# A two-layer graph convolution network: in the first convolution's dense groups, edge attributes become the weights of the matmul and the one-hot table streams past them

## What is computed

```python
def conv(h, W, b):
    m = jnp.concatenate([h[dst], h[src], edge_attr], axis=1) @ W + b
    return jax.ops.segment_sum(m, dst, num_segments=n_nodes)
h = jax.nn.relu(conv(x, W1, b1))
```

## Time and profile before

| | |
|---|---|
| median of 3 runs | 8141.34 us |
| lowest and highest | 8137.03 and 8143.66 us |
| the profiled execution | 8128.06 us |
| its span | 8126.3 us |
| TensorE busy in the span | 6793.0 us (84%) |
| VectorE busy | 4444.9 us (55%) |
| ScalarE busy | 2307.4 us (28%) |
| mean granted clock of TensorE | 0.891 |

### The profile page before, as it was taken

How to read it: one execution, slowest core, us unless ns; L and a number is a source line. 1 busy time by engine, 2 the same in 40 slices (tenths; PEclk the granted TensorE clock), 3 DMA queues, 4 the chain that set the end, 5 groups by cost and what they waited for, 6 DMA issues and landing times. The chain is left out here.

```text
span 8126.3 us, 167963 instructions
## 1 busy us (share of the span) xinstructions
PE 6793.0 (84%) x53896; PEld 5553.6 (68%) x53897; DVE 4444.9 (55%) x5962; ACT 2307.4 (28%) x3815; POOL 5634.3 (69%) x5891
## 2 busy tenths in 40 slices
PE   5999999889997898895788788887868788888886
PEld 4777777788886888885666666665656566666664
DVE  7888886322222222225666666666566666566566
ACT  4878876100000000002222222222232222222223
POOL 4666664477775777774777777777557777777774
PEclk9999998688887888897999998888989889898897
DMA  5666666477776777773222222222232222222222
GB/s 183 238 236 244 236 239 205 167 269 278 284 277 227 287 282 269 272 262 113 72 67 68 72 67 72 68 70 69 59 84 70 70 67 71 69 71 67 72 72 70
DMA packets 415308, 1226.32 MB, mean 151 GB/s; under 512 B 120178, under 2 KB 219852, under 8 KB 366574
## 3 DMA queue, kind: packets, MB, share of 16 engines
q1 hardware_dynamic: 214343, 743.70, 25.6%
q0 software_dynamic: 187712, 233.42, 13.3%
q10 hardware_dynamic: 13160, 248.08, 7.6%
HBM read 943.22 MB, written 281.51 MB: 151 GB/s over the span
## 5 line engine op out<-in xcount | busy, mean ns | idle before, releaser
L1947 POOL DMA_INDIRECT data<-q_rows,idx x3328 | 3160.2, 950 | 1123.5 <-issue 1001.3
L922 POOL DMA_INDIRECT data<-h_parts,idx x2508 | 2427.6, 968 | 1202.3 <-issue 1019.6
L1054 PE MATMUL p_z<-hs,adj 128*128 128x192 bf16 x22442 | 2115.6, 252 | 61.5 <-issue 61.5
L1054 PEld LDWEIGHTS p_z<-hs,adj 128*128 128x128 bf16 x22442 | 1934.6, 100 | 313.4 <-issue 105.3
L2079 ACT COPY back<-p_back 128x1024 f32<-128x1024 f32 x418 | 423.3, 1013 | 2375.2 <-PE p_back L1967 2375.2
L2149 DVE TENSOR_TENSOR_SCAN run<-reset,run,p_turn 128x1024 f32<-128x1024 bf16 x416 | 974.5, 2342 | 147.2 <-PE p_turn L2014 142.8
L1169 ACT CAST adj<-p_count 128x1012 bf16<-128x1012 f32 x836 | 920.0, 1101 | 213.3 <-PE p_count L1040 190.0
L575 DVE TENSOR_TENSOR hot<-p_ramp,ends 128x2048 f32<-128x2048 f32 x416 | 950.0, 2284 | 0.5 <-issue 0.4
L1973 PE MATMUL part<-hot,t 128*128 128x128 f32 x6688 | 910.3, 295 | 44.9 <-issue 44.9
L1973 PEld LDWEIGHTS part<-hot,t 128*128 128x128 f32 x6688 | 879.1, 212 | 45.5 <-issue 45.5
L1978 PE MATMUL part<-hot,back 128*128 128x128 f32 x6688 | 815.1, 275 | 0.0
(11 more groups left out here) (324 smaller groups left out, 6381.9 us busy)
## 6 DMA issues: line engine op xcount, KB each, us to landing
adj<-counted SPq DMA_DIRECT2D x304, 1568.0 KB
counted<-adj ACTq DMA_DIRECT2D x76, 3136.0 KB
reset<-flags SPq DMA_DIRECT2D x208, 512.0 KB
data<-q_rows,idx POOLq DMA_INDIRECT x3328
data<-h_parts,idx POOLq DMA_INDIRECT x2508
feat<-in_ea_blocks SPq DMA_DIRECT2D x208, 128.0 KB
ea<-in_ea_cols SPq DMA_DIRECT2D x154, 88.0 KB
rden<-node_rows SPq DMA_DIRECT2D x50, 256.0 KB
```

Of the source, the lines that this page charges most:

```text
L922: pool.indirect_dma_start(out=data[:, p % HELD, j, 0:PARTS], out_offset=None, in_=table[:, :], in_offset=bass.IndirectOffsetOnAxis(ap=idx[ ...
L1054: mm = pe.matmul(p_z[:, 0:PARTS], adj[:, (q + LAG) % 2, hi, :], hs[:, hi, :], start=(hi == 0), stop=(hi == BLOCKS - 1))
L1947: pool.indirect_dma_start(out=data[:, r, j, :], out_offset=None, in_=q_rows[:, :], in_offset=bass.IndirectOffsetOnAxis(ap=idx[:, r, j:j + ...
```

## The change

In an E group of the first convolution, the operands of the eleven products change places. The attributes (`dense_ea`, 128 edges by 49) are the weights now, and the one-hot table (128 edges by 128 places) streams. The result comes out with features in partitions and places in columns, as `acc` has it, into columns 3P to 4P of the bank of `p_part`. Nothing is left to turn: the copy of ScalarE, the matmul L946 and its waits are gone, and `finish` waits for the products (`s_part`) and reads them where they are. `s_by_feature` is now counted by P groups alone. The P groups and the two later convolutions do what they did. What `further_products` does for edges outside the window is as it was.

```diff
             def products(pos, slot, halfway=None):
                 par = nth[pos] % 2
+                if slot is None:
+                    for j in range(GC):
+                        mm = pe.matmul(p_turned[0:EA, 3 * P:4 * P], dense_ea[:, j, 0:EA], hot[:, par, j, :],
+                                       start=(j == 0), stop=(j == GC - 1))
+                    return mm
                 for j in range(GC):
                     if halfway and j == HALFWAY:
                         halfway()
-                    mm = pe.matmul(p_part[:, columns(pos)], hot[:, par, j, :],
-                                   rows_of_edges(pos, slot, j), start=(j == 0), stop=(j == GC - 1))
+                    mm = pe.matmul(p_part[:, 0:WIDE], hot[:, par, j, :],
+                                   data[:, slot % HELD, j, :], start=(j == 0), stop=(j == GC - 1))
                 return mm
...
-            def by_feature(n):
+            def by_feature():
 
-                if hots[n] not in POS_P:
-                    return pe.matmul(p_turned[0:EA, 2 * P:3 * P], by_place[:, D:], chip.ident[:, :], start=True, stop=True)
                 return pe.matmul(p_turned[0:M, 2 * P:3 * P], by_place[:, 0:M], chip.ident[:, :], start=True, stop=True)
...
             def turn(k, pos):
                 n = nth[pos]
-                if pos in POS_E:
-                    pe.wait_ge(s_by_place, k * NQ + (POS_E.index(pos) + 2))
-                else:
-                    pe.wait_ge(s_by_sum, k * len(POS_P) + ((POS_P.index(pos) if pos >= 0 else -1) + 2))
+                pe.wait_ge(s_by_sum, k * len(POS_P) + (nth_p[pos] + 2))
...
                         if first:
                             between[2] = lambda pos=pos: by_window(k, pos, None)
-                            between[5] = lambda pos=pos: turn(k, pos)
...
                 for i in range(GC):
                     m = q * GC + i
-                    if i == 4:
-                        copy_places(k, POS_E[q])
...
-            def copy_places(k, pos):
-                n = nth[pos]
-                act.wait_ge(s_part, k * H + (H + n + 1))
-                act.wait_ge(s_by_feature, k * H + (n + 1 + BEFORE))
-                gate(act)
-                nc.scalar.copy(by_place[:, D:], p_part[:, PARTS:PARTS + EA]).then_inc(s_by_place, 1)
...
                 to = acc[rows, window(base, 0)]
-                v.wait_ge(s_by_feature, k * H + (n + 2 + BEFORE))
+                if pos in POS_E:
+                    v.wait_ge(s_part, k * H + (H + n + 1))
+                else:
+                    v.wait_ge(s_by_feature, k * len(POS_P) + (nth_p[pos] + 2 + BEFORE))
...
-                v.tensor_tensor(to, to, p_turned[0:at, 2 * P:3 * P], ALU.add).then_inc(s_added, 1)
+                of = slice(3 * P, 4 * P) if pos in POS_E else slice(2 * P, 3 * P)
+                v.tensor_tensor(to, to, p_turned[0:at, of], ALU.add).then_inc(s_added, 1)
```

More of the change, by code:

```diff
@@ L686, in conv_pass @@
     nth[-1] = -1
+    nth_p = {pos: n for n, pos in enumerate(POS_P)}
+    nth_p[-1] = -1
     M = KC if first else D
@@ L928, in _ @@
         def _(pe):
-            columns = lambda pos: slice(0, WIDE) if pos in POS_P else slice(PARTS, PARTS + EA)
-            def rows_of_edges(pos, slot, j):
-                return data[:, slot % HELD, j, :] if slot is not None else dense_ea[:, j, 0:EA]
             def products(pos, slot, halfway=None):
                 par = nth[pos] % 2
+                if slot is None:
[3 more added lines that the diff above has]
+                    return mm
                 for j in range(GC):
@@ L998, in turn @@
                 n = nth[pos]
-                if pos in POS_E:
-                    pe.wait_ge(s_by_place, k * NQ + (POS_E.index(pos) + 2))
-                else:
-                    pe.wait_ge(s_by_sum, k * len(POS_P) + ((POS_P.index(pos) if pos >= 0 else -1) + 2))
+                pe.wait_ge(s_by_sum, k * len(POS_P) + (nth_p[pos] + 2))
                 pe.wait_ge(s_added, k * H + (n + 1 + BEFORE))
                 pe.wait_ge(s_dense_added, k * NQ + (dense_before(pos + 1) + 1))
-                if first:
-                    pe.wait_ge(s_by_place, k * NQ + 1)
-                else:
+                if not first:
                     pe.wait_ge(s_nodes, k + 1)
                 gate(pe)
-                by_feature(n).then_inc(s_by_feature, 1)
+                by_feature().then_inc(s_by_feature, 1)
             def by_window(k, pos, slot, halfway=None):
@@ L1018, in by_window @@
                     pe.wait_ge(s_ea_step, k * (4 * TURN) + (4 * n + 4))
-                    pe.wait_ge(s_by_place, k * NQ + (sum(p < pos for p in POS_E) + 1))
                     pe.wait_ge(s_added, k * H + (n + 1 + BEFORE))
@@ L1097, in _ @@
             pe.wait_ge(s_pick, 1)
+            pe.wait_ge(s_by_place, 1)
             further_windows_of(pe, further)
@@ L1322, in sum_places @@
                 v.wait_ge(s_part, k * H + (H + n + 1))
-                v.wait_ge(s_by_feature, k * H + (n + 1 + BEFORE))
+                v.wait_ge(s_by_feature, k * len(POS_P) + (nth_p[pos] + 1 + BEFORE))
                 if first:
```

## The result

The changed kernel took **8163.9 us** (median of 9 runs, 8157.9 to 8168.12), the kernel before 8140.48 beside it (9 runs, 8137.03 to 8143.66). The ratio is 1.0029, with a 95% interval of 1.0021 to 1.0038: **slower by 0.29%**, 23.4 us. The forecast was 8161.8 us, slower by 0.25%.

A forecast was written before the change was run, and what follows sets the result against it. Each group was bound by a TensorE leg (scatter to sixth counts), then a VectorE leg (to zs). Terms +0.54 and -0.27 gave +0.27 us, times 76 +20.5, on 8128.1 plus 13.3 for the median: 8161.8 us, range 8142 to 8182.

The forecast's parts named there:

- The products: Eleven products on TensorE between scatter and sixth counts: 0.83 us instead of 0.29, +0.54 us per group, costing in full.
- rival (a): No gaps where bf16 products change weight width: +0.05 us a group, 8145 us, not slower; chance 0.15.
- rival (b): Narrow weight loads not hidden behind streams, each product longer: +37 to +54 us, 8178 to 8195 us; chance 0.13.
- The 0.02 us: First narrow weight load of the eleven products, not hidden; read as 0.03 in float32, taken as 0.02 for bf16.
- The turning product on TensorE: Removing this matmul behind the sixth counts frees 0.47 us of TensorE, worth nothing since TensorE waits for zs anyway.
- only the wait for zs grows: TensorE's wait ahead of the scatter for VectorE's sum zs would go from 0.57 to 0.75 us.
- TensorE's later counts wait for VectorE's pairs a little more: Counts behind the sixth would wait slightly longer for VectorE; the 0.57 us wait for zs takes it up.
- The update of acc: On VectorE, no longer waiting for the turning product, it comes 0.45 us after its pair: mean -0.27 us a group.
- The sum: 0.54 - 0.27 = +0.27 us a group, times 76 = +20.5 us; 8161.8 us, 0.25% slower.
- Rival (c): TensorE as the sole bound of the group loop: +0.07 us a group, +5 us, 8147 us; chance 0.05.
- The rival on the faster side: Faster kernel, needing 0.75 us off VectorE's leg, for example by pairs starting sooner: -16 us; chance 0.05.
- The copy on ScalarE: Removing this 206 ns copy in each group was claimed to be worth 0, with no one waiting for it.

The follow-up runs named there:

- Experiment 3: Changed kernel with its attribute tile zero-padded to 128 columns, so the eleven products have 128 weight columns: 8141.56 us, ratio 1.0020 to the kernel before.
- experiment 2: Changed kernel with one count matmul repeated twice behind the sixth counts (`i == 8`): 8148.66 us, ratio 1.0028 to the kernel before.
- Experiment 4: Kernel before with VectorE's update of acc for attributes moved two rounds later, when the turning product is long done: 8149.44 us, ratio 1.0028.
- experiments 1: Changed kernel with one count matmul repeated twice ahead of the sixth counts (`i == 4`): 8184.91 us in one run, kernel before 8126.57 there.

## Why the prediction was right

**The products.** Right, term by term. Taken: 0.10 ahead + 0.02 for the first load + 0.61 + 0.10 behind = 0.83 us, +0.54 against before. Measured: 0.09, 0.02, 0.62 and 0.10, and the leg from the scatter to the sixth counts went from a median of 7.34 to 7.89 us, +0.55. Experiment 3 splits the 0.83 into 0.61 of streaming and 0.22 that the width of 49 adds. With that rival (a), no gaps, falls: they come with bf16 operands too. So does rival (b), loads in the open: only the first of the eleven steps is longer, by 19 ns, and the others are 56 ns with 49 as with 128 weight columns. That the array empties at a change of width is the prediction's picture of the gaps; the runs show their size and place, not what happens in them.

The 0.02 us came partly by luck. The row that it was read from, 0.37 us for the turning product's two rows, holds a wait as well. In that group of before, the counts behind the turning product start 0.82 us after VectorE's copy of p_end does, and they do so in every group of after, where the new wait holds them. In three of four groups of before they start 0.90 or 0.99 us after it, unheld; there the two rows took 0.35 us, and their first step 147 ns where it is 126 with 113 weight columns. So about half of the excess in that row was a wait, and the other half is a real 0.02.

**The turning product on TensorE.** "Worth nothing there, only the wait for zs grows" is right in its first half. The pair added behind the sixth counts (experiment 2) is free, and so was the turning product's 0.47 us. The second half failed. The wait for zs is 0.53 us, where I forecast 0.75. The counts of the seventh round can't start before VectorE has copied p_end, and that holds TensorE for 0.28 to 0.37 us in every group now. In the timeline above it is 0.37, from 625.83 (625.09 + 0.74) to 626.20. The 0.47 us that came free thus became 0.14 of earlier arrival. With VectorE's side 0.26 shorter the wait should be 0.57 + 0.14 - 0.26 = 0.45. The remaining 0.08 is a wait of before that the profile doesn't name, ahead of the counts of the tenth round (the nine matmuls take 0.81 us there, and 0.74 in after):

```profile
619.64 0.90 PE L1054 MATMUL p_z<-hs,adj 128*128 128x192 bf16 x9
620.45 0.19 PE L1037 MATMUL p_end<-high_hot,low_hot 128*128 128x66 f16 x1
```

In all groups of before these counts start 0.146 us behind the end of VectorE's pair, which they need; in after the pair is done sooner, and they don't wait. So the prediction's "TensorE's later counts wait for VectorE's pairs a little more" had the sign wrong. The price of both misses was nil, since these waits lie in the slack.

**The update of acc.** Here one term is mis-sized: I took 0.45 us behind its pair, measured is **0.53** in every kind of group. So this term is -0.18 instead of -0.27. The prediction calls the rows that 0.45 came from "of the same form", but they have 113 partitions, and this update 49. Experiment 4 shows 0.54 for this form in the kernel before, unheld. It was made up, by luck, by terms that I didn't have: the step from to_window's start to ea's fell from 265 to 202 ns, and the copy of p_end starts 0.03 us sooner in the mean. A step further on, behind the cast of code, is 0.01 longer. Net of VectorE's side: -0.26.

**The sum.** Forecast +0.27 us a group; measured +0.30, 22.6 us over 76 groups. That it lies so close owes something to the two terms that made up for the update's. Rival (c), TensorE as the sole bound, falls by experiments 1 and 2. The rival on the faster side had no mechanism, and none appeared.

**The copy on ScalarE** was worth 0, as forecast: neither trace has a wait for it.

**The Trainium skill's rule.** The measured step of the products is 56 ns with 128 streaming columns at 2.4 GHz, with 49 weight columns as with 128, the first step with 49 aside. The page "TensorE: Matmul & The Clock Gate" of the Trainium skill (Back-to-back issue gap) gives about 81 ns for such a matmul with its load; the trace doesn't agree. The same page of the Trainium skill (Weight-path perf modes) keeps the fast load for 128 weights that are not float32. The profile shows a load of 105 ns with 49 columns and of 98 ns in experiment 3, which has 128. Both overlap with the streams, and experiment 3 gained 19 ns at the first product and nothing at the others.

## What to carry to other kernels

Split a loop of two engines that wait for each other into its legs, at the instruction where one hands over to the other, and price an edit by the leg in which it stands; a pair of runs with the same small work put on either side of that point shows the legs at once. A run of matmuls with 49 weight columns between full ones cost 0.21 to 0.22 us in gaps, for two matmuls (the turning product) as for eleven, and padding the eleven to 128 columns took it away; 113 columns cost none ahead of them. A wait that is removed is worth at most what the next one leaves: the edits here that freed time met ScalarE's rounding, a shared tile, the next copy or the scatter's own update. The last of these stood in the code as a wait that the profile put down to "issue": a constant lag behind the end of the instruction that signals, in every group, is what gives such a wait away.

## What the runs showed of the hardware

- Changing from 128 weight columns to 49, and back, costs TensorE 0.09 us ahead, 0.02 at the first narrow matmul and 0.10 behind. With bf16 the starts are 176, 75 and 152 ns apart instead of 82, 56 and 56; with float32 (the turning product of before) 176, 147 and 205 instead of 82, 126 and 109. It shows at each change and not at each matmul. Eight matmuls of L1054 ahead of L947, with 113 weight columns, take 0.65 us, 82 ns each: no gap there.
- The same VectorE instruction (L1362, 128x1078 in f16) took 0.50 us in nearly all places, and 0.54 to 0.64 in some, mostly the same ones of a kernel and others in the next kernel. The cause is open; it cost experiment 3 about 0.09 us a group.
- The update of acc starts 0.43 to 0.47 us behind its pair where it has 113 partitions, and 0.53 to 0.54 where it has 49, no wait being shown. With 49 it starts 0.03 us behind the end of its pair in every kernel that doesn't hold it longer, with 113 it starts 0.03 to 0.09 before that end. Whether the form or the place makes the difference isn't told apart.
- One chip ran every kernel in 12,890 to 13,064 us, 1.60 times the others' time. Its mean granted clock was 0.744 instead of 0.89, which alone would make a factor of 1.20 at most; the rest were stalls without a releaser on the core. In between, nine matmuls of L1048 took their 0.74 us as elsewhere. Three kernels that are 0.2 to 0.7% slower than before on the other chips were level with it there, and a fourth, 0.41% slower elsewhere, was 0.66% faster. Why is not settled.
